# Edge attention in a graph layer: Q rows and exponents handled once a pair of batches instead of once a batch

## What is computed

```python
q = (feat @ Wq.T + bq).reshape(n, H, HD)
k = (feat @ Wk.T + bk).reshape(n, H, HD)
v = (feat @ Wv.T + bv).reshape(n, H, HD)
score = jnp.einsum('ehd,ehd->eh', q[edge_dst], k[edge_src])
score = jnp.clip(score / math.sqrt(HD), -10.0, 10.0)
ex = jnp.exp(score - smax[edge_dst])          # smax: maximum over a node's edges
den = jax.ops.segment_sum(ex, edge_dst, num_segments=n)
alpha = ex / den[edge_dst]
wv = jax.ops.segment_sum(alpha[:, :, None] * v[edge_src], edge_dst, num_segments=n).reshape(n, C)
x = feat + wv @ Wp.T + bp
h = _layernorm(x, ln_g, ln_b)
h = jax.nn.gelu(h @ W1.T + b1, approximate=False) @ W2.T + b2
out = _layernorm(feat + x + h)                # all in float32
```

## Time and profile before

| | us |
|---|---|
| median of 3 runs | 1149.14 |
| lowest and highest | 1146.2, 1150.38 |
| span of the profiled execution | 1484.0 |

### The profile page before, as it was taken

How to read it: one execution, slowest core, us unless ns; L and a number is a source line. 1 busy time by engine, 2 the same in 40 slices (tenths; PEclk the granted TensorE clock), 3 DMA queues, 4 the chain that set the end, 5 groups by cost and what they waited for, 6 DMA issues and landing times.

```text
span 1484.0 us, 26187 instructions
## 1 busy us (share of the span) xinstructions
PE 1135.0 (76%) x6188; PEld 724.7 (49%) x6188; DVE 954.9 (64%) x1539; ACT 672.3 (45%) x1936; POOL 912.0 (61%) x1550
## 2 busy tenths in 40 slices
PE   8956778776977778777866876768877967877887
PEld 6823335454544454444544544544544544544566
DVE  6806676677676576666666666657667657666573
ACT  3212235455544545535544544535544535544543
POOL 4584667677776566766667566666667566666500
PEclk9976668999898788888798788887897788878699
DMA  9985877768777667776677676676677676676510
GB/s 328 314 253 178 254 227 225 229 199 253 214 220 225 203 188 222 227 232 196 197 237 208 191 230 197 199 236 179 206 236 209 191 238 196 197 225 199 180 54 23
DMA packets 154887, 312.25 MB, mean 210 GB/s; under 512 B 32200, under 2 KB 73126, under 8 KB 154791
## 3 DMA queue, kind: packets, MB, share of 16 engines
q0 software_dynamic: 61536, 200.85, 45.6%
q1 hardware_dynamic: 93254, 110.43, 23.3%
HBM read 270.02 MB, written 41.16 MB: 210 GB/s over the span
## 4 chain that ended last, share of the span: by engine, by line
PE 42%; another core or an unknown queue 23%; ACT 14%; issue 14%; DVE 5%; ACTq 1%; DVEq 0%; DMA 0%; SPq 0%
PE bank L483 9%; PE bank L503 7%; PE bank L951 5%; PE quad L875 4%; PE bank L930 3%; PE quad L942 3%; PE bank L977 3%; PE bank L964 2%; ACT hid L496 2%; PE bank L455 2%; ACT hid L491 1%; DVE kv L1636 1%; ACT hn L1276 1%; ACT staged L1217 1%
## 5 line engine op out<-in xcount | busy, mean ns | idle before, releaser
L401 POOL DMA_INDIRECT kv<-kv_rows,src_sb x750 | 721.5, 962 | 443.4 <-PE bank L951 212.1
L1616 DVE TENSOR_TENSOR prod<-kv,quad 128x1024 f32<-128x1024 f32 x196 | 239.3, 1221 | 346.6 <-remote 228.0
L1636 DVE TENSOR_TENSOR kv<-kv,bank 128x1024 f32<-128x1024 f32 x196 | 238.2, 1215 | 16.7 <-ACT kv L1209 16.7
L1623 DVE TENSOR_REDUCE score<-prod 128x32 f32<-128x1024 f32 x196 | 237.7, 1213 | 0.8
L483 PE MATMUL bank<-hT,w_sb 128*128 128x256 f32 x736 | 212.4, 440 | 17.9 <-ACT hid L491 17.9
L951 PE MATMUL bank<-kv,onehot 128*32 128x264 f32 x1568 | 150.1, 442 | 83.2 <-issue 49.5
L503 PE MATMUL bank<-w_sb,hid 128*128 128x256 f32 x736 | 205.3, 435 | 0.9 <-issue 0.7
L483 PEld LDWEIGHTS bank<-hT,w_sb 128*128 128x128 f32 x736 | 159.6, 222 | 52.5 <-issue 11.6
L942 PE MATMUL quad<-qwin,onehotT 32*128 32x256 f32 x1568 | 108.8, 354 | 95.7 <-issue 54.1
L503 PEld LDWEIGHTS bank<-w_sb,hid 128*128 128x128 f32 x736 | 159.8, 223 | 34.5 <-issue 8.7
L930 PE MATMUL bank<-staged,place 128*128 128x264 f32 x196 | 81.5, 502 | 113.8 <-ACT staged L1217 76.0
(11 more groups left out here) (164 smaller groups left out, 1421.0 us busy)
## 6 DMA issues: line engine op xcount, KB each, us to landing
qwin<-q_rows SPq DMA_DIRECT2D x392, 64.0 KB
dst_rows<-edge_dstT SPq DMA_DIRECT2D x50, 256.0 KB
q_rows<-q_next SPq DMA_DIRECT2D x25, 512.0 KB
kv_rows<-kv_out SPq DMA_DIRECT2D x24, 512.0 KB
kv<-kv_rows,src_sb POOLq DMA_INDIRECT x750
agg_rows<-acc_sb SPq DMA_DIRECT2D x98, 82.5 KB
xT_sb<-xT SPq DMA_DIRECT2D x25, 256.0 KB, 5.4
xq_sb<-xT SPq DMA_DIRECT2D x25, 256.0 KB
```

The source lines that it names most:

```text
L401: return nc.gpsimd.indirect_dma_start(out=rows, out_offset=None, in_=kv_dram, in_offset=bass.IndirectOffsetOnAxis(ap=index, axis=0))
L1616: nc.vector.tensor_tensor(prod[:, slot % 2].rearrange("p (i c) -> p i c", c=C), kv[:, slot, :, 0:C], quad[:, :, 0:C], ALU.mult).then_inc(s ...
L1623: nc.vector.tensor_reduce(score[:, slot % 2], prod[:, slot % 2].rearrange("p (h d) -> p h d", d=HD), AX.X, ALU.add).then_inc(s_score, 1)
L1636: nc.vector.tensor_tensor(kv[:, slot, :, C:2 * C].rearrange("p i (h d) -> p i h d", d=HD), kv[:, slot, :, C:2 * C].rearrange("p i (h d) -> ...
```

## The change

The banks of `quad` are 512 columns wide, and the Q rows of the pair's second batch go into columns 256 to 511. `q_rows` is called once a pair, waits until both products of the pair before are done and issues sixteen matmuls with one semaphore increment at the end; `s_qe` counts pairs. VectorE's order for a pair becomes: both products, onehots(p), weight and scores in turn for the two batches (weights of pair p-1, scores of pair p), one clip over both batches, then the node steps of both slots with output between them. ScalarE runs `exponents` once a pair over both batches (again two activations, twice as wide) at the head of the pair's slots; stage stays at the end of the odd slot. TensorE's order: q_rows(p+1), merge(p-2), node steps of the even slot, both sums of p-1, node steps of the odd slot. The copy of the projected x rows into `kv` moves from slot 6 to slot 5. Loops run over four half turns (`HALF_TURN`) instead of eight slots.

```diff
--- before.py
+++ after.py
@@ -618,7 +618,7 @@
 
             def load_q_windows(p, slot):
                 if exists(p - 4, PAIRS):
-                    sp.wait_ge(s_qe, 2 * p - 6)
+                    sp.wait_ge(s_qe, p - 3)
                 base = pair_base(p)
                 for i in range(TILES):
                     sp.dma_start(row_parts(qwin[WIN * i:WIN * (i + 1), slot]),
@@ -930,17 +930,18 @@
                 nc.tensor.matmul(bank4[:, 0:ACC], place[:, slot % 2], staged[:, slot % 2], start=True, stop=True)\
                     .then_inc(s_mrg, 1)
 
-            def q_rows(n, slot, p, uses):
-                pe.wait_ge(s_qwin[slot // 2], 64 * uses)
+            def q_rows(p, buffer, uses):
+                pe.wait_ge(s_qwin[buffer], 64 * uses)
                 pe.wait_ge(s_ohT, p + 1)
-                if exists(n - 1, BATCHES):
-                    pe.wait_ge(s_prod, n)
-                cols = slice(slot % 2 * P, (slot % 2 + 1) * P)
-                for part in range(2):
-                    for i in range(TILES):
-                        rows = slice(WIN * i, WIN * (i + 1))
-                        last = nc.tensor.matmul(quad[:, i, 0:C], onehotT[rows, slot // 2, cols],
-                                                qwin[rows, slot // 2, part], start=(part == 0), stop=(part == 1))
+                if exists(p - 1, PAIRS):
+                    pe.wait_ge(s_prod, 2 * p)
+                for b in range(2):
+                    for part in range(2):
+                        for i in range(TILES):
+                            rows = slice(WIN * i, WIN * (i + 1))
+                            last = nc.tensor.matmul(quad[:, i, b * C:(b + 1) * C],
+                                                    onehotT[rows, buffer, b * P:(b + 1) * P],
+                                                    qwin[rows, buffer, part], start=(part == 0), stop=(part == 1))
                 last.then_inc(s_qe, 1)
 
             def sums(n, slot, p):
@@ -987,7 +988,7 @@
                 pe.wait_ge(s_xgTc, X_FIRST)
                 project_x(1, hT[:, :, P:SB], bank4)
                 pe.wait_ge(s_qb, 2 * EARLY_Q)
-                q_rows(0, 0, 0, 1)
+                q_rows(0, 0, 1)
                 pe.wait_ge(s_xkv, 1)
                 project_x(2, xgT)
 
@@ -1033,18 +1034,17 @@
                     last.then_inc(f_f2, 1)
 
             def edges(turn, r, parity):
-                for i in range(SLOTS):
-                    n = SLOTS * turn + i
-                    if exists(n + 1, BATCHES):
-                        q_rows(n + 1, (i + 1) % SLOTS, 4 * turn + (i + 1) // 2, turn + (i + 1) // SLOTS + 1)
-                    if i % 2 == 0 and exists(4 * turn + i // 2 - 2, PAIRS):
-                        merge(4 * turn + i // 2 - 2, (i // 2 + 2) % 4)
-                    if i != 5:
-                        node_steps(turn, i)
-                    if exists(n - 2, BATCHES):
-                        sums(n - 2, (i - 2) % SLOTS, 4 * turn + (i - 2) // 2)
-                    if i == 5:
-                        node_steps(turn, i)
+                for j in range(HALF_TURN):
+                    p = 4 * turn + j
+                    if exists(p + 1, PAIRS):
+                        q_rows(p + 1, (j + 1) % 4, turn + (j + 1) // 4 + 1)
+                    if exists(p - 2, PAIRS):
+                        merge(p - 2, (j + 2) % 4)
+                    node_steps(turn, 2 * j)
+                    for b in range(2):
+                        if exists(p - 1, PAIRS):
+                            sums(2 * p - 2 + b, (2 * j - 2 + b) % SLOTS, p - 1)
+                    node_steps(turn, 2 * j + 1)
 
             def last_ffn1(s, pair, bank):
                 pe.wait_ge(f_hT, s + 1)
@@ -1197,17 +1197,17 @@
                                      ACT.Abs, bias=minus_start[:, bass.ds(p, 1)]).then_inc(s_dist, 1)
                 act.wait_ge(s_dist, p + 1)
                 if exists(p - 4, PAIRS):
-                    act.wait_ge(s_qe, 2 * p - 6)
+                    act.wait_ge(s_qe, p - 3)
                 nc.scalar.activation(onehotT[:, slot], distance[:], ACT.Relu, scale=-1.0, bias=one_col[:])                    .then_inc(s_ohT, 1)
 
-            def exponent(n, slot):
-                act.wait_ge(s_clip, n + 1)
-                if exists(n - 1, BATCHES):
-                    act.wait_ge(s_ev, n)
-                first = EX_COL + slot % 2 * TILES * H
-                nc.scalar.activation(bank5[:, first:first + TILES * H], clipped[:, slot % 2], ACT.Exp, scale=SCALE)
-                nc.scalar.activation(kv[:, slot, :, 2 * C:KVW],
-                                     clipped[:, slot % 2].rearrange("p (i h) -> p i h", h=H),
+            def exponents(p, buffer):
+                act.wait_ge(s_clip, p + 1)
+                if exists(p - 1, PAIRS):
+                    act.wait_ge(s_ev, 2 * p)
+                nc.scalar.activation(bank5[:, EX_COL:EX_COL + 2 * TILES * H],
+                                     clipped[:].rearrange("p b x -> p (b x)"), ACT.Exp, scale=SCALE)
+                nc.scalar.activation(kv[:, 2 * buffer:2 * buffer + 2, :, 2 * C:KVW],
+                                     clipped[:].rearrange("p b (i h) -> p b i h", h=H),
                                      ACT.Exp, scale=SCALE).then_inc(s_exp, 1)
 
             def stage(p, slot):
@@ -1343,7 +1343,7 @@
                 early_x = x_early(turn, i)
                 if early_x and i % 2 == 1:
                     copy_x_kv(early_x, X_TILES[early_x][0:2], X_TILE)
-                if i + 1 == X_SLOT and x_turn(turn):
+                if i + 2 == X_SLOT and x_turn(turn):
                     copy_x_kv(x_index(turn, X_SLOT), (turn, X_SLOT), X_TILE)
                 if i == 2 and exists(turn, Q_UNITS - EARLY_Q):
                     copy_q(turn)
@@ -1371,26 +1371,26 @@
                     norm_out(turn - 1)
 
             def edges(turn, r, parity):
-                for i in range(SLOTS):
-                    n = SLOTS * turn + i
-                    if exists(n - 1, BATCHES):
-                        exponent(n - 1, (i - 1) % SLOTS)
-                    done = 4 * turn + i // 2 - 2
-                    if i % 2 == 0 and exists(done, PAIRS):
-                        copy_sums(done, (i // 2 + 2) % 4)
-                    if i % 2 == 0 and exists(done + 1, PAIRS):
-                        select_carry(done + 1, (i // 2 + 3) % 4)
-                    if isinstance(turn, int) and n == BATCHES:
+                for j in range(HALF_TURN):
+                    p = 4 * turn + j
+                    if exists(p - 1, PAIRS):
+                        exponents(p - 1, (j - 1) % 4)
+                    if exists(p - 2, PAIRS):
+                        copy_sums(p - 2, (j + 2) % 4)
+                    if exists(p - 1, PAIRS):
+                        select_carry(p - 1, (j + 3) % 4)
+                    if isinstance(turn, int) and p == PAIRS:
                         gelu(SUPERBLOCKS - 3, range(FC // 2))
-                    node_steps(turn, i)
-                    if i % 2 == 1 and exists(done + 1, PAIRS):
-                        stage(done + 1, (i // 2 + 3) % 4)
-                    if isinstance(turn, int) and n == BATCHES + 1:
+                    node_steps(turn, 2 * j)
+                    if exists(p + 2, PAIRS):
+                        transposed_onehots(p + 2, (j + 2) % 4, turn + j // 2 + 1)
+                    if j == 3 and exists(turn - 1, SUPERBLOCKS):
+                        norm_h(turn - 1)
+                    node_steps(turn, 2 * j + 1)
+                    if exists(p - 1, PAIRS):
+                        stage(p - 1, (j + 3) % 4)
+                    if isinstance(turn, int) and p == PAIRS:
                         gelu(SUPERBLOCKS - 3, range(FC // 2, FC))
-                    if i % 2 == 0 and exists(4 * turn + i // 2 + 2, PAIRS):
-                        transposed_onehots(4 * turn + i // 2 + 2, (i // 2 + 2) % 4, turn + i // 4 + 1)
-                    if i == 6 and exists(turn - 1, SUPERBLOCKS):
-                        norm_h(turn - 1)
 
             act.wait_ge(s_const, 9)
             nc.scalar.activation(minus_ident[:], ident[:], ACT.Copy, scale=-1.0)
@@ -1596,7 +1596,7 @@
 
             def onehots(p, slot):
                 if exists(p - 1, PAIRS):
-                    dve.wait_ge(s_exp, 2 * p - 1)
+                    dve.wait_ge(s_exp, p)
                 if exists(p - 4, PAIRS):
                     dve.wait_ge(s_part, 2 * p - 6)
                 nc.vector.tensor_tensor(onehot[:, slot],
@@ -1606,32 +1606,33 @@
                                         .broadcast_to([P, PAIR_TILES, WIN]),
                                         ALU.is_equal)
 
-            def products(n, slot, turn):
+            def products(n, slot, turn, p):
                 dve.wait_ge(s_kv[slot], kv_done(turn, slot) - 16 * (TILES - gathered(n)))
                 if x_tiles(turn, slot):
                     dve.wait_ge(s_xkv, x_index(turn, slot) + 1)
-                dve.wait_ge(s_qe, n + 1)
```

(62 more changed lines are left out.)

## The result

The changed kernel takes 1261.35 us (median; 1257.1 to 1271.24) against 1149.46: a ratio of 1.0986, 95% interval 1.0932 to 1.1039. It is 112 us slower; 1300 was forecast, with 1190 to 1390 around it.

What follows compares the result with a forecast made beforehand. GpSimd's gathers, with VectorE close behind, were taken to set a 39.8 us turn. 1149 us plus 117 for the new loop and 33 for the ring of gathers gave 1299, rounded to 1300 us, range 1190 to 1390.

Steps and rivals of the forecast that it cites:

- GpSimd sets the turn, the chain has room: Kernel before: GpSimd's gathers at 1.33 us set a 39.8 us turn, VectorE close behind; weighting waits for exponents only 16.7 us.
- Fewer instructions: One clip a pair instead of two on VectorE: 1.5 us a turn, at most 37 us, only if VectorE is the limit.
- The common part and the pairs: Exponents to exponents: 5.5 us common to all pairs, plus each pair's node steps, giving 10.8, 9.0, 12.2 and 13.0 us.
- Pair 2: Common 5.5 us plus 6.7 for x-row projection, its copy, moments and table load before the exponents: 12.2 us.
- The clock, +1.5: TensorE's terms in the loop run slower at the lower granted clock: 1.5 us more a turn.
- the pace, -1.4: The unprofiled turn seems to run at 0.97 of the profile's pace: 1.4 us less a turn.
- The ring, +33 us: Key/value slots free later and GpSimd gets two at once, delaying gathers: 1.5 us a turn beyond the loop, +33 us.
- the loop: Exponents, weightings, sums, stage, next exponents close once a pair without slack: 45.1 us a turn, +117 us; chance 0.75.
- The signs: Expected in the changed profile: one-hots wait for exponents, Q-row waits shrink, GpSimd idles more, VectorE's busy time falls 20 to 35 us.
- (a): Rival: node steps' hand-overs are ready early, GpSimd still sets 39.8 us a turn, time 1149 us; chance 0.08.
- (b): Rival: VectorE sets the turn, the loop no longer than its work; up to 37 us gained, 1112 to 1135; chance 0.07.
- (c): Rival: the ring of gathers limits too; with gathers landing in 25 us, turn 51 us, time 1390 us; chance 0.10.

Runs made afterwards that it cites:

- before's second trace: The kernel before, unchanged, traced again: median 1152.63 us, span 1150.8 us, against a span of 1484.0 us in its first trace.

## Why the prediction was right, point by point

- *GpSimd sets the turn, the chain has room.* Right, and shown by before's second trace (4.0 us of waits in 1.33 us steps). It was argued from a trace in which GpSimd waits for much, because the times left no room for those waits. The size was a little off: 40.9 us a turn, not 39.8. The experiment without pauses bears it out: 0.07 to 0.08 us less a gather made 51 us. The 175 us outside the products, taken from the first trace, contained some 18 us of late start, which belong to slow transfers; 157 is right.
- *Fewer instructions.* VectorE's busy time fell by 17 us (950.3 to 933.6), under the 20 to 35 named as a sign, and none of it reached the time, as said.
- *The common part and the pairs.* Pairs 0, 1 and 3 took 10.7, 8.6 and 12.9 us for 10.8, 9.0 and 13.0. In pair 3 one sees each link on ScalarE: norm_h waits for the roots, scale_h for TensorE's transposes, then norm_out, stage and exponents in a row.

```profile
720.00 1.09 ACT L535 ACTIVATE hn<-x,root 128x256 f32<-128x256 f32 x2 [6.78 <-DVE root L531]
722.30 1.02 ACT L475 ACTIVATE hT<-bank,lngb_sb 128x256 f32<-128x256 f32 x2 [1.21 <-PE bank L469]
723.22 1.08 ACT L535 ACTIVATE y_out<-z,root 128x256 f32<-128x256 f32 x2
724.20 0.38 ACT L1217 ACTIVATE staged<-bank 128x264 f32<-128x264 f32 x1
724.47 0.22 ACT L1207 ACTIVATE bank<-clipped 128x64 f32<-128x64 f32 x1
```

- *Pair 2* took 13.9 us for 12.2, and the trace splits these 1.7. TensorE in pair 2 of the turn that is shown, and of the next turn:

```profile
699.98 3.48 PE L455 MATMUL bank<-wp_sb,wvT 128*128 128x256 f32 x8
703.39 1.24 PE L952 MATMUL bank<-kv,onehot 128*32 128x264 f32 x16
...
704.99 1.98 PE L978 MATMUL bank<-wqkv_in,xgT 128*128 128x512 f32 x4
...
746.06 1.99 PE L455 MATMUL bank<-wp_sb,wvT 128*128 128x256 f32 x8
747.99 1.10 PE L952 MATMUL bank<-kv,onehot 128*32 128x264 f32 x16
...
749.44 1.98 PE L978 MATMUL bank<-wqkv_in,xgT 128*128 128x512 f32 x4
```

The same stretches, with the busy time of each engine, the granted clock (0.57 and 1.00), the DMA share and GB/s:

```profile
700.00:704.00 4.00, 4.00 (x17) 2.60 (x20) 3.66 (x5) 3.94 (x6) 3.46 (x6) 0.57 1.03 394
746.10:750.10 4.00, 4.00 (x28) 2.41 (x28) 3.97 (x6) 3.94 (x5) 3.52 (x7) 1.00 1.03 400
```

I let the last sums follow the weighting at once and left out the output projection, which stands ahead of them in TensorE's order. Seen from the one-hots, the second weighting ends at 3.8 us in both turns. At the full clock the output projection ends at 3.9, the sums of both batches come behind it as one run of 16 and end at 5.0, where I had them end at 4.6; the pair takes 12.5 us, 0.3 more than forecast. At the lower clock the projection takes 3.5 us and the sums end at 6.6; the pair takes 14.2. In 7 of twenty turns TensorE is at the lower clock already at the merge behind the Q rows, and the pair takes 15.7. The mean is 1.4 us above the 12.5 of the full clock.

Then ScalarE, as forecast:

```profile
707.09 0.60 ACT L1257 ACTIVATE kv<-bank 128x512 f32<-128x512 f32 x1 [2.65 <-PE bank L978]
...
709.84 0.37 ACT L1217 ACTIVATE staged<-bank 128x264 f32<-128x264 f32 x1
710.23 1.28 ACT L1207 ACT_TABLE_LOAD   x1
711.52 0.23 ACT L1207 ACTIVATE bank<-clipped 128x64 f32<-128x64 f32 x1
```

The load begins 0.02 us after stage ends, and the exponents start 0.01 us behind it. The drain of some 1380 ns that the Trainium skill (ScalarE: Activation LUTs, What ACT_TABLE_LOAD costs) adds to a load isn't seen here.
- *The clock, +1.5, and the pace, -1.4.* They cancelled in the sum. The clock's term was right in size: pair 2 alone loses 1.4 us a turn to the lower clock, as just shown. The correction of the pace to 0.97 was wrong: GpSimd's step is 1.33 us in the good trace too, and with the right outside part nothing has to be corrected.
- *The ring, +33 us.* This term failed. The periods of the loop as measured already give the time: 22 x (46.1 - 40.9) = 114 us, and 112 were measured. The 28 us from issue to product came from the trace with slow transfers. GpSimd does wait 102.5 us for freed slots, but behind the loop, not ahead of it: VectorE's products wait for x rows (40.1 us, ScalarE), and none of their waits in the trace ends with a gather.
- *The signs.* One-hots wait for the exponents of pairs 0, 2 and 3, and not of pair 1, 74 times in 98: right for where. The sizes in the turn shown are 1.4, 3.2 and 2.1 us, for 2 in pair 0 and 3 to 4 in the others. The waits for Q rows: 12.5 us, all of it one wait, from 29.4 in before's second trace.
- *The rivals.* (a) and (b) needed the loop to be shorter than 9.95 or 9.2 us a pair; it is 11.5. (c) did not occur, since no product waited for a gather; whether it describes the slow chip is open, as said there.

Of 1300 - 1261 = 39 us, 33 are the ring. The turn of before was taken 1.1 us too short and that of the change 1.0 us (45.1 for 46.1), so these two nearly cancel, which is luck: 22 x 5.3 = 117 us were forecast for the loop, and 112 measured. The mechanism, the loop with its four sums, was right without it.

## What to carry to other kernels

When work for two steps is merged, follow each in-order engine once round and add up what now stands between an output and its next use; a loop that had a free slot in it can close, and then every node of it counts, on engines that are half idle. Here one call moved ahead of a wait gave back 108 of 112 us. And before an engine downstream is relieved, see which engine paces: here it was GpSimd at a constant 1.33 us a gather, so 17 us less on VectorE could give nothing. A constant step tells this better than a busy share does: without the pauses GpSimd was busy 68% and still set the turn, at 1.25 us a gather. And where periods fall into groups, sort them by what differs (here the granted clock) before taking a mean or a median.

## What the runs showed of the hardware

- The kernel before took 1148 to 1149 us on three chips and 1494 us on a fourth. Traces with times like the first have 271 GB/s over the span, those like the last about 210. The compute durations are the same (a product 1.22 us in both). Whether the chip itself is slower, or something else used its memory at the time, isn't shown. A trace whose span is 30% over the median can be of such an execution, and its waits for transfers then say nothing of the timed runs; its durations do.
- The pause of 0.20 us behind each gather costs 51 us on a chip where GpSimd paces, and 0.5% on the slow one (0.9949; 0.9907 to 0.999). A gather of 0.95 us is followed by the next after 0.30 us where nothing stands between them, and with the pause by 0.37 in all: 1.25 us against 1.33.
- One and the same output projection took 1.99 us at a granted clock of 1.00 and 3.48 to 3.78 where the clock was at or near half of it.
